# First attention: the two column sums of a stage move from slots 3 and 7 to slots 5 and 13, directly behind V's products

## What is computed

```python
q = (x @ Wq).reshape(B, S, H, D).transpose(0, 2, 1, 3)      # B 8, S 256, H 16, D 64
k = (c @ Wk).reshape(B, N, D, H).transpose(0, 3, 2, 1)      # N 1601
v = (c @ Wv).reshape(B, N, D, H).transpose(0, 3, 1, 2)
mask = jnp.all(c == 0, axis=-1)[:, None, None, :]
scores = jnp.where(mask, -jnp.inf, jnp.einsum('bhsd,bhdn->bhsn', q, k) * D ** -0.5)
att = jax.nn.softmax(scores, axis=-1)                       # the denominator: sum over n of exp
out = jnp.einsum('bhsn,bhnd->bhsd', att, v)
x = x + out.transpose(0, 2, 1, 3).reshape(B, S, H * D) @ Wo
```

## Time and profile before

| | us |
|---|---|
| median of 3 runs | 2127.22 |
| lowest, highest | 2125.81, 2131.59 |
| the profiled execution: time | 2127.05 |
| its span, from the first to the last instruction | 2125.3 |
| PE busy | 1982.3 (93%) |
| DVE busy | 1693.7 (80%) |
| POOL busy | 1161.7 (55%) |
| ACT busy | 1065.4 (50%) |

### The profile page before, as it was taken

The page is one execution under the profiler, slowest core; times in us unless marked ns, Lnnn a source line. Parts: engine busy times, 40 slices in busy tenths (PEclk is TensorE's granted clock), DMA queues, the critical chain, the costliest instruction groups (busy, mean ns, idle before and its releaser), DMA issues. The chain is left out here.

```text
span 2125.3 us, 35171 instructions
## 1 busy us (share of the span) xinstructions
PE 1982.3 (93%) x10757; PEld 1451.8 (68%) x10757; DVE 1693.7 (80%) x4048; ACT 1065.4 (50%) x1493; POOL 1161.7 (55%) x624
## 2 busy tenths in 40 slices
PE   5999999999999999999999999999966899779995
PEld 4677777777677777767777777777645688557774
DVE  7898888888887888888888888888647777757765
ACT  3445445453545545453545545454534799644442
POOL 0275756657575655757575666657764445314340
PEclk9899999999999999999999999999986999879997
DMA  3000000000000000000000000000000212112210
GB/s 95 1 1 17 1 4 17 1 1 4 18 1 4 2 16 1 4 18 1 1 4 17 1 4 1 1 1 1 1 6 16 91 60 75 38 49 63 74 35 24
DMA packets 54855, 40.84 MB, mean 19 GB/s; under 512 B 2500, under 2 KB 51596, under 8 KB 53644
## 3 DMA queue, kind: packets, MB, share of 16 engines
q1 hardware_dynamic: 54668, 38.57, 6.1%
HBM read 37.45 MB, written 1.11 MB: 18 GB/s over the span
## 5 line engine op out<-in xcount | busy, mean ns | idle before, releaser
L374 POOL TENSOR_TENSOR a_den<-a_den,a_probs 128x1024 f32<-128x1024 f32 x352 | 844.3, 2402 | 332.2 <-ACT a_probs L572 331.8
L572 ACT ACTIVATE a_probs<-a_probs,a_mask_col 128x1024 f32<-128x1024 f32 x416 | 478.8, 1151 | 571.8 <-DVE a_probs L741 571.7
L741 DVE TENSOR_TENSOR a_probs<-a_scores,a_shift 128x512 f32<-128x512 f32 x832 | 565.0, 685 | 160.1 <-PE a_scores L399 138.8
L682 DVE CUSTOM_DVE_ANT_0 a_work<-a_work,a_mask_row 128x400 f32<-128x400 f32 (+1 forms) x1024 | 571.7, 589 | 47.7 <-PE a_work L431 47.3
L479 PE MATMUL a_pv<-a_probs,a_V 128*64 128x256 f32 x3328 | 405.2, 385 | 1.0 <-ACT a_probs L572 0.9
L397 PE MATMUL a_scores<-a_Q_hi,a_cT_hi 128*128 128x512 f32 x832 | 345.7, 415 | 6.4 <-DVE a_probs L741 4.6
L431 PE MATMUL a_work<-a_cT_hi,a_Q_hi 128*128 128x400 f32 (+1 forms) x1024 | 328.0, 369 | 2.4
L398 PE MATMUL a_scores<-a_Q_lo,a_cT_hi 128*128 128x512 f32 x832 | 328.1, 394 | 0.0
L399 PE MATMUL a_scores<-a_Q_hi,a_cT_lo 128*128 128x512 f32 x832 | 326.6, 393 | 0.0
L479 PEld LDWEIGHTS a_pv<-a_probs,a_V 128*64 128x64 f32 x3328 | 220.5, 136 | 150.3 <-issue 39.1
L431 PEld LDWEIGHTS a_work<-a_cT_hi,a_Q_hi 128*128 128x128 f32 x1024 | 193.7, 190 | 98.3 <-issue 43.1
(11 more groups left out here) (319 smaller groups left out, 2849.4 us busy)
## 6 DMA issues: line engine op xcount, KB each, us to landing
m_gate_rows<-gate_scratch SPq DMA_DIRECT2D x8, 1024.0 KB, 4.9
a_c_nat<-in_ctx_dram SPq DMA_DIRECT2D x8, 768.0 KB
b_c_in<-in_ctx_dram SPq DMA_DIRECT2D x8, 768.0 KB
b_c_nat<-in_ctx_dram SPq DMA_DIRECT2D x8, 768.0 KB
m_w_raw<-in_L_ffn_W_dram SPq DMA_DIRECT2D x16, 256.0 KB, 5.0
a_acc<-in_x_dram SPq DMA_DIRECT2D x8, 128.0 KB, 2.1
out_dram<-tokens SPq DMA_DIRECT2D x4, 256.0 KB, 2.3
a_V<-in_L_xattn_Wq_dram SPq DMA_DIRECT2D x1, 512.0 KB, 6.6
```

The source lines that it names most:

```text
L374: nc.gpsimd.tensor_tensor(half, so_far, probs[:, buffer(c, j), :], ALU.add).then_inc(den_added, 1)
L572: nc.scalar.activation(probs[:, buffer(c, j), :], probs[:, buffer(c, j), :], ACT.Exp, bias=mask_col[:, c // 2 % 2, j // 2:j // 2 + 1]).the ...
L682: nc.vector.tensor_tensor_reduce(out=X[:, bank, :w], in0=X[:, bank, :w], in1=mask_row[:, off:off + w], scale=1.0, scalar=-3e38, op0=ALU.ad ...
L741: nc.vector.tensor_tensor(probs[:, buffer(c, j), pair * 2 * S:(pair + 1) * 2 * S], Sc[:, pair, :], shift[:, first:first + 2 * S], ALU.add) ...
```

## The change

The two den items of a stage stand in other slots. Everything else is as it was: the same instructions with the same operands, apart from which of the four banks an item takes, since the banks are numbered by the order of the slots.

```diff
@@ plan(c, tail, prep)
         if tail:
-            slots[3].append(("den", 0))
-            slots[7].append(("den", 1))
+            slots[5].append(("den", 0))
+            slots[13].append(("den", 1))
             for i in range(8):
                 slots[RECIP[i]].append(("recip", i))
```

## The result

The changed kernel takes 2142.73 us (median of 6 runs, 2138.22 to 2143.89), the kernel before 2128.34 us (median of 6, 2125.81 to 2131.59). The ratio is 1.0067, with a 95% interval of 1.0055 to 1.0078: 14.4 us slower. The profiled execution took 2141.87 us, 14.8 more than that of before.

What follows compares the result with a forecast made beforehand. DVE sets the pace up to V's products of steps 6 and 7, PE behind them. Delays 7 x 1.04 (odd) + 7 x 0.59 (even) + 1.2 (last) = 12.6 us on 2127.05; forecast 2139.5 us, range 2129 to 2146.

Steps and rivals of the forecast that it cites:

- What an isolated group costs: On PE, a den group alone takes 1.21 us, beside V's products 0.87: 0.34 us less for each group.
- Part 1: First den group from slot 3 to 5: costs nothing, gives PE 0.34 us in even stages; odd 0 to 0.2 later.
- Part 2: Second den group from slot 7 to 13: V's products, group, POOL's add and handovers delay DVE's step 5 subtraction; chain 5.37 us.
- Even stages: Stages 2, 4, ... 14: DVE's subtraction of step 5 comes 0.59 us later.
- Odd stages: Stages 1, 3, ... 13, which prepare the next batch row: DVE's subtraction of step 5 comes 1.04 us later.
- The last stage: Stage 15, which prepares nothing: DVE's subtraction of step 5 comes 1.5 us later, part taken back, leaving 1.2.
- A: Rival: PE is the bound throughout and the new wait is covered; 9.9 us gained, 2117 us; chance 0.08.
- B: Rival: DVE's subtraction of step 5 does not wait for POOL's add; 4.8 us less, 2122 us; chance 0.08.
- C: Rival: delay partly made good by unseen DVE idle time or PE reserve; half of 12.6, about 2133 us; chance 0.10.
- D: Rival: POOL is not back in step for the next subtractions; 2145 to 2152 us; chance 0.06.
- Points 1 to 4: Profile after: gapless 0.87 us groups; POOL's second add behind group; 15 DVE waits; only V's steps 2-3 to 6-7 longer.
- Point 5: Profile after: odd stages near 98.2 us instead of 97.2, even ones 0.6 us longer.

Runs made afterwards that it cites:

- e3: Changed kernel (groups in slots 5 and 13) with the second half of den doubled, used in turn by stages: 2122.70 us against 2128.14 before, ratio 0.9967.
- e1: Kernel before with only the first den group moved, to slot 5, the second staying in slot 7: 2126.23 us against 2128.14, ratio 0.9986.
- e8: Changed kernel with reciprocals spread over slots 8 to 29, normalisation and Wo product later: 2132.23 us against 2126.69 for the kernel before, ratio 1.0021.
- e4: Den groups directly ahead of V's products (end of slots 4 and 12), against the kernel before: 2124.61 us against 2128.14, ratio 0.9985.
- e11: Changed kernel with POOL's second add of each stage from 1 on cut to 512 columns: 2125.87 us against 2127.44 for the kernel before, ratio 0.9993.

## Why the prediction was right

The sign, the place and nearly the size came out: 2139.5 us forecast, 2142.7 measured, range 2129 to 2146.

- **What an isolated group costs.** Forecast 1.21 us alone and 0.87 beside V's products. In the changed kernel V's products and the group of stage 2 together take from 279.79 + 0.23 to 283.15 less some 0.18 for the product of 400 columns ahead of it, 2.95 us; the earlier trace rows gave 2.94. And e3 shortens an even stage by 0.71 us, two gaps of 0.34 to 0.36. That it is the form of the array, as the prediction says, is argued: the groups differ from the scores around them in the type too (plain fp32 against the rounded fp32 of the scores), and no run changes one alone. The product with Wo in the kernel before speaks for the form; it is plain fp32 in the 128x128 form, 16 instructions as V's products are:

```profile
300.35 0.39 PE L399 MATMUL a_scores<-a_Q_hi,a_cT_lo 128*128 128x512 f32 x1
300.58 1.95 PE L451 MATMUL a_work<-a_Wo,a_outT 128*128 128x128 f32 x16
302.28 0.43 PE L431 MATMUL a_work<-a_cT_hi,a_Q_hi 128*128 128x400 f32 x1
302.55 0.40 PE L397 MATMUL a_scores<-a_Q_hi,a_cT_hi 128*128 128x512 f32 x1
```

Counted as above, from 300.35 + 0.23 to 302.55 - 0.18, it takes 1.79 us, and V's products 2.07. It is no proof, since its instructions have 128 columns and V's 256.

- **Part 1 costs nothing.** Right. e1 is 2 to 3 us faster. POOL's first add came behind the group at 275.29 instead of behind the exponential, but its reader is not waiting. In odd stages the 0.2 us taken for the mask's wait came out as 0.12 in e1.
- **Part 2, the chain.** Forecast 2.81 + 0.09 + 2.38 + 0.09 = 5.37 us, measured 5.42, with 0.17 for the handover from PE to POOL and 0.04 for that from POOL to DVE in the place of twice 0.09.
- **Even stages.** Forecast 0.59 us, measured 0.58: DVE's wait is 1.44, and without it the stages would be shorter than before, as e3 showed.
- **Odd stages.** Forecast 1.04, measured 1.14.
- **The last stage.** Forecast 1.2, measured 1.78. This is the term that was mis-sized. V's products of step 3 came about 0.2 us later than taken (they moved up by 0.83 us and not 1.0), and the 0.3 us that I let DVE make good behind the subtraction were not made good. e8 shows the same from another side: what lies behind the wait does not absorb it.
- **The rest.** The sum was 12.6 us and the stages give 13.8. The medians differ by 14.4 and the profiled executions by 14.8, where the loop's first turn adds 1.6. The forecast of 2139.5 also starts from 2127 us, and the six runs of the kernel before have a median of 2128.34, so 1.1 of the 3.2 us that it lacks come from there.
- **The rivals.** A (all of PE's saving counts, 2117) and the rule of the Trainium skill behind it, "TensorEngine Tiling (Array Packing)", Key Properties, that a change of tiling mode drains TensorE: the gap is there, and taking it out is worth 0.7 us in an even stage when nothing else waits (e3), but the rule does not see who reads the group. B (the wait doesn't bind, 2122) is what e3 and e4 make true by other means: 2122.7 and 2124.6. C (half made good) and D (POOL falls behind further on) did not come; from V's products of step 7 to the stage's end all intervals agree with those of before within 0.03 us.
- **What the profile was to show.** Points 1 to 4 hold: no gap ahead of the group (V's products at 280.12, the group at 281.90), POOL's add behind the group and not behind the exponential, 15 new waits of 1.44 (even), 1.01 (odd) and 2.71 us (last), and only the way from V's products of step 3 to those of step 5 longer. Point 5 names 98.2 us for stage 1 in place of 97.20, counted between V's products of step 1; so counted it is 97.86. That count leaves out the stage's own start, which the group's leaving shortens by 0.7 us, and takes in that of the next stage, which it shortens by 1.2; the difference of 0.5 us I had not set against it.

## What to carry to other kernels

Ask of a moved instruction first who reads its result and who may overwrite its source, and not only what it costs on its own engine: here a saving of 0.34 us on PE for each group was paid with a chain of 5.4 us that ran over two other engines to the queue that set the pace. The slack of such a chain can be worked out ahead from starts of rows (the add ended 1.67 us ahead of its reader, and was moved by more than that). Moves of this kind are best made after the reader has been freed, by a second buffer (e3, 5 to 7 us faster than before) or by an order in which the short group goes ahead of the long one (e4, 3 us); and which stage gains is to be asked for each kind of stage apart.

## What the runs showed of the hardware

- An isolated group of fp32 products in the 128x64 form among products in the 128x128 form costs PE about 0.34 us more than beside another such group (1.21 + 2.07 against 2.94 us; 0.71 for two in e3), and no engine's row shows it as work. That the change of form makes it is likely (1.79 against 2.07 us for the product with Wo) and not shown.
- From the end of PE's last product, as the profile models it, to POOL's start it took 0.17 us (0.18 in e11), from ACT's end to POOL 0.09, and from POOL's end to DVE 0.04.
- POOL's add of 128x1024 in fp32 takes 2.38 to 2.40 us, and that of 128x512 1.29 (e11).
- Where the loop turns, the profiles lose 2.4 to 5.6 us (stages 5 and 9 against the other odd stages of the loop), and the loss differs by up to 3 us from profile to profile, by which differences of this size in single profiles are to be distrusted.
